# Selective-scan kernel on one core: one product and one scan of 2048 elements per group of states in place of two each

## What is computed

```python
def step(h, inp):                                   # over the 512 tokens of a batch
    d_t, B_t, C_t, u_t = inp
    dA = jnp.exp(d_t[..., None] * A)                # (256 channels, 16 states)
    h = h * dA + (d_t * u_t)[..., None] * B_t[:, None, :]
    y = jnp.einsum('bdn,bn->bd', h, C_t)
    return (h, y)
...
y = (ys + xi * Dp) * silu(z)
return y @ out_w.T
...
x = x + mamba_both_directions(xn) + experts(xn)     # each token goes to one expert
```

## Time and profile before

| what | value |
|---|---|
| median of 3 runs | 901.2 us (898.68 to 901.28) |
| profiled execution, its own time | 899.89 us |
| its span, first to last instruction | 898.0 us |
| busy: DVE | 877.3 us (98%) |
| busy: POOL | 795.4 us (89%) |
| busy: PE | 746.1 us (83%) |
| busy: ACT | 699.7 us (78%) |
| TensorE clock granted, mean | 0.903 of full speed |
| DVE products with B, 256 of 1024 elements | 300.7 us |
| DVE scans, 256 of 1024 elements | 570.7 us |
| POOL products with C, 255 of 1024 elements | 596.1 us |

### The profile page before, as it was taken

One profiled execution on the slowest core, in us unless ns is written; L12 is line 12 of the kernel. 1 busy time (PEld: TensorE's weight loads), 2 busy tenths in 40 slices (PEclk: granted clock), 3 DMA queues, 4 the chain that ended last, 5 costly groups with the idle time before them and its releaser, 6 DMA issues.

```text
span 898.0 us, 10752 instructions
## 1 busy us (share of the span) xinstructions
PE 746.1 (83%) x3067; PEld 333.8 (37%) x3067; DVE 877.3 (98%) x631; ACT 699.7 (78%) x1191; POOL 795.4 (89%) x446
## 2 busy tenths in 40 slices
PE   8889877978889888799888987889878879889476
PEld 5334322332235444354443543445333432324122
DVE  6999999999999999999999999999999999999987
ACT  5999956865679889988989889997979977576550
POOL 0788789999999989889899988999898999999995
PEclk9969878796999989999899998989999899979579
DMA  7895353245545545553546636455554434453400
GB/s 235 228 281 120 110 118 109 91 106 159 149 112 171 130 160 146 183 134 101 181 116 192 165 72 211 124 185 130 182 139 111 135 87 169 106 172 69 103 0 13
DMA packets 90989, 123.60 MB, mean 138 GB/s; under 512 B 7978, under 2 KB 63275, under 8 KB 86963
## 3 DMA queue, kind: packets, MB, share of 16 engines
q1 hardware_dynamic: 88882, 118.72, 46.7%
q0 software_dynamic: 2048, 4.20, 1.5%
HBM read 75.57 MB, written 14.29 MB: 100 GB/s over the span
## 4 chain that ended last, share of the span: by engine, by line
issue 21%; POOL 15%; PE 10%; ACT 5%; DVE 3%; POOLq 0%; DMA 0%; ACTq 0%
POOL hs L1544 10%; POOL gu_w L1516 2%; PE front L607 2%; DVE hs L1305 2%; ACT L1099 2%; PE in_b L670 1%; PE y L704 1%; ACT dA L1090 1%; DVE in_b L1286 1%; POOL yg L1526 1%; PE y L695 1%; PE moe L860 1%; PE moe L878 1%; PE front L784 1%; DVE hs L1303 1%
## 5 line engine op out<-in xcount | busy, mean ns | idle before, releaser
L1544 POOL TENSOR_TENSOR hs<-hs,C_rep 128x1024 f32<-128x1024 f32 x255 | 596.1, 2358 | 43.3 <-DVE hs L1305 27.4
L1090 ACT ACTIVATE dA<-delta_rep,A_sb 128x511 f32<-128x511 f32 x512 | 335.7, 718 | 8.5 <-DMA delta_rep<-tmpA 5.3
L1286 DVE TENSOR_TENSOR in_b<-in_b,B_rep 128x1024 f32<-128x1024 f32 x256 | 300.7, 1222 | 6.0 <-PE in_b L670 5.4
L1305 DVE TENSOR_TENSOR_SCAN hs<-dA,in_b 128x1024 f32<-128x1024 f32 x128 | 285.4, 2271 | 0.4 <-PE y L704 0.4
L1303 DVE TENSOR_TENSOR_SCAN hs<-dA,in_b 128x1024 f32<-128x1024 f32 x128 | 285.3, 2273 | 0.1
L670 PE MATMUL in_b<-du,cst 128*128 128x512 f32 x256 | 156.9, 698 | 59.8 <-DVE hs L1305 44.9
L704 PE MATMUL y<-hs,cst 128*32 128x512 f32 x1016 | 133.3, 642 | 12.6 <-POOL hs L1544 12.5
L607 PE MATMUL front<-xpad,w_in 128*128 128x512 f32 x248 | 118.8, 614 | 8.1 <-ACT xi L1015 6.2
L1099 ACT ACT_TABLE_LOAD x71 | 91.1, 1283 | 13.3 <-PE moe L860 7.3
L670 PEld LDWEIGHTS in_b<-du,cst 128*128 128x128 f32 x256 | 46.6, 214 | 134.5 <-issue 131.0
L607 PEld LDWEIGHTS front<-xpad,w_in 128*128 128x128 f32 x248 | 46.8, 197 | 64.9 <-issue 50.9
(11 more groups left out here) (171 smaller groups left out, 816.7 us busy)
## 6 DMA issues: line engine op xcount, KB each, us to landing
delta_rep<-tmpA SPq DMA_DIRECT2D x126, 256.0 KB, 3.8
C_rep<-dbc_scratch SPq DMA_DIRECT2D x16, 1024.0 KB, 7.5
B_rep<-dbc_scratch SPq DMA_DIRECT2D x15, 1024.0 KB, 5.2
gu_w<-in_gate_up SPq DMA_DIRECT2D x39, 384.0 KB, 3.6
dn_w<-in_down SPq DMA_DIRECT2D x39, 192.0 KB, 2.9
xs<-sorted_tokens SPq DMA_DIRECT2D x39, 64.0 KB, 3.8
sorted_ffn<-ys SPq DMA_DIRECT2D x39, 64.0 KB, 2.6
sorted_tokens<-up_f SPq DMA_DIRECT2D x9, 256.0 KB, 4.6
```

The costliest lines, as they stand in the source:

```text
L1090: i = e.activation(dA[:, m % NA, r * L + 1:(r + 1) * L], src, ACT.Exp, scale=A_sb[:, d, 2 * p + jj, RH * rh + r:RH * rh + r + 1])
L1286: e.tensor_tensor(to, in_b[:, 2 + 2 * odd, :].unsqueeze(1).broadcast_to([P, RH, L]), by, ALU.mult).then_inc(dve_mult, 1)
L1305: e.tensor_tensor_scan(to[:, ::-1], a[:, 1:n + 1][:, ::-1], b[:, ::-1], 0.0, ALU.mult, ALU.add).then_inc(dve_scan, 1)
L1544: e.tensor_tensor(hs[:, m % NH, :], hs[:, m % NH, :], C_rep[:, u % 2, RH * rh:RH * rh + RH, :].rearrange("p r t -> p (r t)"), ALU.mult).th ...
```

## The change

Each group now gets one product of 2048 elements and one scan of 2048 elements. The five banks stay; an even group has du in bank 0 and uses banks 0 to 3, an odd group has du in bank 4 and uses banks 1 to 4, and the bank that holds du is written last. The decays of a group lie side by side in one slot of `dA` (3 slots of 4 rows in place of 6 of 2), the ring `hs` has 14 halves and is filled in pairs. The semaphores still count halves: the product adds 2 to `dve_mult` and the scan adds 2 to `dve_scan`. The product waits for all scans up to the group before (`dve_scan >= m`), the scan for both halves of the decays and of its own group's product (`act_decay` and `dve_mult >= m + 2`). Only the first group's product is still in two halves, the second half first. The other edits make room in SBUF: a mask for the routing is loaded later into a tile that is free then, and the statistics of the norm share a tile with the logits. POOL's products with C and ACT's decays keep their size and count.

```diff
-NA, NH = 6, 13
+NA, NH = 6, 14
...
-        dA = sb("dA", [P, NA, RH * L + 1])
+        dA = sb("dA", [P, NA // 2, R * L + 1])
...
+                if m == CLEAR + NTILE // KB + 1:
+                    e.dma_start(not_first, consts[:, C_NOTFIRST:]).then_inc(in_mask, 16)
...
                         if b >= 1:
                             e.wait_ge(pe_base, b)
+                        else:
+                            e.wait_ge(act_route, 2)
                         e.dma_start(x_in[:, :, :], by_batch(x, b)).then_inc(in_base, 16)
...
-                e.matmul(in_b[:, 2 + 2 * (j % 2), :], spread(j), du[:, du_slot(v, j // 4), :],
+                e.matmul(in_b[:, 4 * (j % 2), :], spread(j), du[:, du_slot(v, j // 4), :],
                          start=True, stop=True).then_inc(pe_du, 1)
...
                 for r in range(RH):
-                    i = e.activation(dA[:, m % NA, r * L + 1:(r + 1) * L], src, ACT.Exp,
+                    at = (RH * rh + r) * L
+                    i = e.activation(dA[:, m // 2 % (NA // 2), at + 1:at + L], src, ACT.Exp,
...
-            def du_B(m):
+            def du_B(m, rows=slice(0, R)):
...
                 if m >= 2:
-                    e.wait_ge(dve_scan, m - 1)
...
+                    e.wait_ge(dve_scan, m)
+                n = rows.stop - rows.start
+                to, by = in_b[:, odd + rows.start:odd + rows.stop, :], B_rep[:, u % 2, rows, :]
+                if not odd:
+                    to, by = to[:, ::-1, :], by[:, ::-1, :]
+                e.tensor_tensor(to, in_b[:, 4 * odd, :].unsqueeze(1).broadcast_to([P, n, L]), by,
+                                ALU.mult).then_inc(dve_mult, n // RH)
...
             def scan(m):
...
                 if m >= NH:
-                    e.wait_ge(pe_y, (m - NH) // 8 * 2 + (m - NH) % 2 + 1)
+                    e.wait_ge(pe_y, (m - NH) // 8 * 2 + 2)
...
-                e.wait_ge(act_decay, m + 1)
-                e.wait_ge(dve_mult, m + 1)
...
+                e.wait_ge(act_decay, m + 2)
+                e.wait_ge(dve_mult, m + 2)
+                n = R * L
...
-                    e.tensor_tensor_scan(to, a[:, 0:n], b, 0.0, ALU.mult, ALU.add).then_inc(dve_scan, 1)
+                    e.tensor_tensor_scan(to, a[:, 0:n], b, 0.0, ALU.mult, ALU.add).then_inc(dve_scan, 2)
...
-                    if m < LAST and m % 2 == 0:
-                        du_B(m + i)
-                    elif m < LAST:
-                        scan(m - 1 + i)
+                    if m == 0:
+                        du_B(0, slice(RH * (1 - i), RH * (2 - i)))
+                    elif i == 0 and m < LAST and m % 2 == 0:
+                        du_B(m)
+                    elif i == 0 and m < LAST:
+                        scan(m - 1)
```

More of the change, by code:

```diff
@@ L42 @@
             (UNITS - 2, 0): 218, (UNITS - 2, 1): 219, (UNITS - 1, 0): 232, (UNITS - 1, 1): 235}
-C_ID, C_TRI, C_SEL, C_IOTA, C_THR, C_NOTFIRST, C_TILE = 0, 128, 256, 288, 296, 328, 584
+C_ID, C_TRI, C_SEL, C_IOTA, C_THR, C_TILE = 0, 128, 256, 288, 296, 328
 C_SPREAD = C_TILE + NTILE
@@ L47 @@
 C_END = C_FOUR + P
+C_NOTFIRST = C_END
 NCOL = 14 + NTAP
@@ L195, in mamba_moe_kernel @@
         xn2 = sb("xn2", [P, KB, H])
-        stats = sb("stats", [P, (NB - 1) * KB, 6])
         moments = sb("moments", [P, NB, KB, 2])
@@ L224, in mamba_moe_kernel @@
         xin = attn_in
+        not_first = x_in[:, :, :].rearrange("p k h -> p (k h)")[:, 0:E * NBLK]
         late_in = (xn[:, 0, :, :], attn_in[:, 0, :, :])
@@ L228, in mamba_moe_kernel @@
         logits = sb("logits", [P, NBLK, E])
+        stats = logits[:, :, :].rearrange("p k e -> p (k e)")[:, 0:(NB - 1) * KB * 6].rearrange("p (n s) -> p n s", s=6)
         pos_u = sb("pos_u", [P, NBLK], U32)
@@ L280, in mamba_moe_kernel @@
         in_base, out_attn = sem("in_base"), sem("out_attn")
+        in_mask = sem("in_mask")
         out_clear = sem("out_clear")
@@ L400, in sync_program @@
                 e.dma_start(x_rest[:, n, :], rest[:, n, :]).then_inc(in_all_x[k], 16)
-            e.dma_start(cst[:, P:], consts[:, P:]).then_inc(in_back, 16)
+            e.dma_start(cst[:, P:], consts[:, P:C_END]).then_inc(in_back, 16)
             e.dma_start(outw_t, out_w).then_inc(in_out, 16)
@@ L432, in load_bc @@
                 if v == 0:
-                    for h in range(2):
+                    for h in (1, 0):
                         e.dma_start(B_rep[:, 0, RH * h:RH * h + RH, :].rearrange("p r t -> p (r t)"),
@@ L497, in sync_program @@
                     store_norm(c)
+                if m == CLEAR + NTILE // KB + 1:
+                    e.dma_start(not_first, consts[:, C_NOTFIRST:]).then_inc(in_mask, 16)
                 if m == FOUR - 8:
-                    e.dma_start(four, consts[:, C_FOUR:]).then_inc(in_four, 16)
+                    e.dma_start(four, consts[:, C_FOUR:C_END]).then_inc(in_four, 16)
                 for b in range(NB):
@@ L727, in last_sums @@
                         wait_c(e, n)
-                    i = e.matmul(in_b[r * DD:(r + 1) * DD, 2, :], sel, hs[:, n % NH, r % RH * L:(r % RH + 1) * L],
+                    i = e.matmul(in_b[r * DD:(r + 1) * DD, 0, :], sel, hs[:, n % NH, r % RH * L:(r % RH + 1) * L],
                                  start=True, stop=True, skip_group_check=True)
@@ L1143, in scalar_program @@
                     e.copy(M[:, 0:256], logits[:, :, :].rearrange("p k e -> p (k e)")).then_inc(act_route, 1)
-                    e.copy(M[:, 256:512], cst[:, C_NOTFIRST:C_NOTFIRST + 256]).then_inc(act_route, 1)
+                    e.wait_ge(in_mask, 16)
+                    e.copy(M[:, 256:512], not_first).then_inc(act_route, 1)
                 for v in fronts(m, -7, -7):
@@ L1273, in du_B @@
                 e.wait_ge(pe_du, J * u + s // 2 + 1)
-                if m < 2:
-                    e.wait_ge(in_half[m], 16)
+                if m == 0:
+                    e.wait_ge(in_half[rows.start // RH], 16)
                 elif s == 0:
@@ L1289, in scan @@
+                n = rows.stop - rows.start
[4 more added lines that the diff above has]
+                                ALU.mult).then_inc(dve_mult, n // RH)
             def scan(m):
                 u, s = divmod(m, NSTEP)
-                half, odd = s % 2, s // 2 % 2
+                odd = s // 2 % 2
@@ L1302, in scan @@
+                e.wait_ge(dve_mult, m + 2)
+                n = R * L
+                b = in_b[:, odd:odd + R, :].rearrange("p r t -> p (r t)")
+                a = dA[:, m // 2 % (NA // 2), :]
+                to = hs[:, m % NH:m % NH + 2, :].rearrange("p h t -> p (h t)")
                 if u % 2 == 0:
-                    e.tensor_tensor_scan(to, a[:, 0:n], b, 0.0, ALU.mult, ALU.add).then_inc(dve_scan, 1)
+                    e.tensor_tensor_scan(to, a[:, 0:n], b, 0.0, ALU.mult, ALU.add).then_inc(dve_scan, 2)
@@ L1304, in scan @@
                 else:
                     e.tensor_tensor_scan(to[:, ::-1], a[:, 1:n + 1][:, ::-1], b[:, ::-1], 0.0,
-                                         ALU.mult, ALU.add).then_inc(dve_scan, 1)
+                                         ALU.mult, ALU.add).then_inc(dve_scan, 2)
             def times_C(m):
@@ L1337, in last_gate @@
                     n = slice(k * L // 2, (k + 1) * L // 2)
-                    e.tensor_tensor(yg_four[:, n], in_b[:, 2, n], z_four[:, n], ALU.mult).then_inc(dve_last_gate, 1)
+                    e.tensor_tensor(yg_four[:, n], in_b[:, 0, n], z_four[:, n], ALU.mult).then_inc(dve_last_gate, 1)
             def route(part):
@@ L1405, in vector_program @@
             e.memset(xpad[:, L + NTAP - 1:], 0.0).then_inc(dve_const, 1)
-            e.memset(dA[:, :, 0:RH * L + 1:L], 0.0).then_inc(dve_const, 1)
+            e.memset(dA[:, :, 0:R * L + 1:L], 0.0).then_inc(dve_const, 1)
             e.wait_ge(in_x[0], 16)
@@ L1570, in shape_constants @@
     import numpy as np
-    c = np.zeros((P, C_END), np.float32)
+    c = np.zeros((P, C_NOTFIRST + E * NBLK), np.float32)
     c[:, C_ID:C_ID + P] = np.eye(P)
```

## The result

The changed kernel takes 943.4 us (median of 4 runs, 941.4 to 945.2), the kernel before 899.9 us beside it: a ratio of 1.0486, with a 95% interval of 1.0451 to 1.0520. The change makes the kernel 4.9% slower. The forecast was 918.0 us with a range of 911 to 926: the direction was right and the size less than half. The profiled execution of the changed kernel took 941.4 us, with a span of 939.6 where it was 898.0.

What follows compares the result with a forecast made beforehand. DVE was taken to bound the kernel. From 899.89 us, groups +18.3, start +0.2, end +2.2, idle time taken up -3.4 and decays +0.8 gave +18.1, so 918.0 us, range 911 to 926.

Steps and rivals of the forecast that it cites:

- What bounds the kernel: In the loop over the 128 groups: DVE, busy 98% of the span, sets the pace at 6.62 us a group.
- The lengths of the merged tiles: Per group on DVE: product 2.286 us and scan 4.398 us, together 6.684 us, from slopes between shapes.
- the bound for steeper slopes: Per group on DVE: slopes 0.3% steeper would make the group 0.155 us longer in place of 0.144.
- The new waits: Between dependent product and scan on DVE: overlap is lost, a group takes 6.764 us, +18.3 us over 127 groups.
- 0.04 twice a group: On DVE: 0.04 us from an instruction's end to the dependent next one's start, twice a group, 0.08 us together.
- at the start: In the first group, still with two products: its scan starts later and the link behind adds 0.07, +0.2 us.
- The rival that the waits hide: In DVE's groups: dependent instructions start as early as independent ones, 6.50 us a group, 891 us in all; chance 0.07.
- the one that every instruction costs its whole duration already: In DVE's groups: fewer instructions save 0.31 us a group, about 874 us in all; chance 0.01.
- Idle time that a slower DVE takes up: Late in the loop, where POOL is behind: DVE's waits shrink, -3.4 us, bounds 0 and -4.3.
- the new decay waits: At DVE's scans: four second halves of ACT's decays come late; less shrinking earlier idle times, +0.8 us, -2.7 to +4.9.
- the rival that it is all taken up: In the loop: all 7 us of DVE's idle time vanish and no decay is late, 913.6 us; chance 0.15.
- The end: Behind the last scan: POOL's last product with C delays PE's last sums to 2.59 us from 0.41, +2.2 us.

## Why the prediction was right and wrong

**What bounds the kernel** was right: the loop runs at DVE's pace, and a cost per group on DVE came through in full.

**The lengths of the merged tiles** were right within 0.6%: 6.720 us where the slopes gave 6.684. That is 0.036 us a group, 4.6 us of the 47; the bound for steeper slopes had allowed 0.011.

**The new waits** are the step that failed. The mechanism was right, both waits are exposed and the overlap of 0.09 us is lost. The term "0.04 twice a group" was mis-sized: it measured 0.132 twice, 0.185 us a group and **23.5 us** in all. That is nearly the whole miss of 23.4 us in the profiled execution (941.4 against 918.0); the other terms nearly cancel. I took the link from two pairs of the trace in which the second instruction carries its wait for the first. The product and the scan had their waits for DVE elsewhere, and the trace of before shows it, in a view that I did not read for this (the lines of these two waits, in the kernel before):

```profile
L1279 DVEq EVENT_SEMAPHORE  x254: 21/21/50, 29.4 to 883.5; - x127
...
L1297 DVEq EVENT_SEMAPHORE  x256: 21/50/1734, 26.0 to 885.8; - x128
```

These are the kernel before's waits for the scan and for the product, as instructions of the sequencer. There they ran while the instruction ahead was still working and cost nothing; the price showed once they stood directly behind the instruction that they waited for. And the change added a second reason: by adding 2 the product and the scan lost the wait that they had carried. It went to the sequencer, where the product's instruction now holds two waits and not one; that of the scan held two before. Counting by 1 gave back only the 0.03 us of the product's; most of the price is the place of the wait. The kernel that has the forecast's link, the one that counts groups and writes the own wait first, measures 922.8 us, inside the range. Its span says the same by terms, +22.1 us where +18.1 was forecast: 127 x 0.171 = 21.7 for the groups (18.3 forecast; the tiles add 4.6, and the links of 0.034 in place of 0.04 take off 1.5), 2.3 at the end (2.2), 0.35 at the start (0.2), and -2.2 of idle time (-2.6).

**The rival that the waits hide** fell, and so did the one that every instruction costs its whole duration already: a semaphore between two instructions does cost, 0.12 us against two without one when it is carried, 0.22 us when it is not. The rule of the Trainium skill beside the second rival ("VectorE: DVE Perf Modes", "The DRAIN you can't avoid") says of its own measurement that "the semaphore costs nothing extra here"; here it costs 0.12 us at least.

**Idle time that a slower DVE takes up.** The forecast took up part of it, -2.6 us with the new decay waits; it was -8.5 (the rival that it is all taken up had -7.0). Since a group was 0.37 us longer and not 0.14, the rival "the slack takes up all" came true in this term: the waits of DVE in the changed kernel name PE's du with 0.3 us, and ACT's decays with 0.2. In the run whose group was near the forecast's, with 6.788 us, the waits were as forecast in kind (waits of DVE: us in total, times, longest):

```profile
DVE in_b L1292 <- PE in_b L677: 3.3, 4, 1.5
...
DVE hs L1312 <- ACT dA L1098: 2.1, 2, 1.1
```

The decays were late for halves 91 and 155, by 1.0 and 1.1 us where 0.9 and 1.2 were forecast; the one for half 119 did not show.

**The end** cost 2.60 us where 2.2 was forecast, but not along the way I gave: that the number is near is luck. The timeline of the changed kernel, which answers to the earlier trace rows, and behind it two rows of the kernel before that the earlier trace rows does not show:

```profile
924.63 4.42 DVE L1312 TENSOR_TENSOR_SCAN hs<-dA,in_b 128x2048 f32<-128x2048 f32 x1
...
929.09 1.23 DVE L1319 TENSOR_TENSOR hs<-hs,C_rep 128x1024 f32<-128x1024 f32 x1
929.13 3.40 POOL L1553 TENSOR_TENSOR hs<-hs,C_rep 128x1024 f32<-128x1024 f32 x1 [1.10 <-DVE hs L1312]
...
932.03 1.16 PE L791 MATMUL front<-w_out,yg 128*128 128x128 f32 x8
...
933.12 1.07 PE L735 MATMUL in_b<-hs,cst 128*32 128x512 f32 x8
```

```profile
890.15 1.31 DVE L1312 TENSOR_TENSOR hs<-hs,C_rep 128x1024 f32<-128x1024 f32 x1
...
891.57 0.17 PEld L728 LDWEIGHTS in_b<-hs,cst 128*32 128x32 f32 x4 [0.91 <-issue]
```

PE's last sums start 4.07 us behind the scan, not 2.59: POOL's product takes 3.40 us in place of 2.36, beside DVE's product with C, and PE begins 0.59 us behind POOL's end and not 0.15, since it is still at a projection (line 791). The sums then take 1.07 us in place of 2.13. In the kernel before the row of 2.13 us held a wait: the last four of its eight matmuls load their weights from 891.57 on, behind DVE's product with C of the last half, which ends at 891.46. So their end, 2.54 us behind the last scan (892.65 - 890.11), hung there on DVE's product and not on the start that I went by, and the forecast's own path would have cost 2.59 + 1.07 - 2.54 = 1.1 us and not 2.2. The two misses nearly cancel. With both merges and carried waits the time behind the last scan is 10.2 us, with the scans in halves 8.6, before 7.9: most of this term comes from the pairing.

## What to carry to other kernels

Before a wait is put directly behind the instruction that it waits for, look not only at pairs of such instructions, but at where the wait itself stands: as an instruction of the sequencer in the trace, or inside the waiting instruction. Write the wait that opens last first among an instruction's waits and let counters add 1: here the two together took about 20 us out of the merged kernel. With carried waits the merge of the products saved 0.07 us a group (6.85 to 6.79) and that of the scans 0.05 (6.83 to 6.79). A rotation without direct waits, as in the kernel before, saves 0.12 us against a carried link at each of two links, and is worth more than the merges: 6.62 us a group against 6.79.

## What the runs showed of the hardware

The link between two dependent DVE instructions has sizes that I had not expected: 0.034 us when the waiting instruction carries the wait, 0.10 or 0.13 us with the wait (alone, or with a second one behind it) in an instruction of the sequencer, 0.09 when the wait that opens last stands last in it; without a dependence the next one starts 0.08 to 0.09 us before the end. A product or scan that adds 2 to its counter carried no wait in either run where they add 2 (the changed kernel, and the one with only the waits reordered); why stays open.

DVE and POOL got in each other's way in two places, where the kernel before kept them nearly apart. One is the end above. The other is the cast of the tokens' positions in the routing (timeline of the changed kernel):

```profile
140.71 4.67 POOL L1553 TENSOR_TENSOR hs<-hs,C_rep 128x1024 f32<-128x1024 f32 x2 [2.68 <-DVE hs L1312]
...
141.29 1.81 DVE L1404 CAST pos_u<-small 128x32 uint32<-128x32 f32 x1
```

The cast has 32 elements, took 0.15 us in the kernel before, and here ends at 143.10, just when the first of POOL's two products (140.71 + 2.34 = 143.05) is done. In every run with the scan merged it took 1.81 to 1.83 us. With the product merged alone and the scan in halves it took 0.15 us again, POOL being idle at that moment. The Trainium skill's page "SBUF — State Buffer", in "Who interferes with whom", says that casts in a fast mode, and DVE instructions with two inputs in SBUF, share a pair of ports with GpSimd, and that the one that comes second is blocked for the other's whole instruction. Both rows agree with it: the cast ended with POOL's product, and POOL's 3.40 us are 1.04 over its 2.36, beside a DVE product that ran 1.19 us after POOL's start. A third row fits less well: in the kernel before DVE's product with C started at 890.15, 0.22 us ahead of the end of POOL's, and took 1.31 us, only 0.08 over the 1.23. No run here separates the ports from another cause.

In three groups of the changed kernel (at 480, 655 and 830 us) about 0.36 us more lie between scan and product, 1.1 us in all, with no other engine named. Counted in the trace's records, the sequencer's among them, the three products are the 448th, 576th and 704th of DVE's list, 128 apart. Gaps of about this size stand at the same three places of the list in the run that only reorders the waits (476, 650 and 823 us), and at the 320th, 448th and 576th in the run that only counts groups (370, 593 and 816 us). In the merged runs whose links are carried nothing shows at these places. What the gaps are stays open.
